# A cross-attention and mixture-of-experts kernel: GpSimd's descriptor memory set to 2048 bytes per partition

## The reference: what is computed

```python
x = x + xattn(layernorm(x), ctx, ctx)        # per position: 16x16 scores of heads, softmax, times v
xf = layernorm(x).reshape(-1, 256)           # 4096 rows
top1 = argmax(xf @ gate_w.T + gate_b)        # one of 8 experts
for e in range(8):
    y = relu(xf @ w1[e].T + b1[e]) @ w2[e].T + b2[e]      # 256 -> 1024 -> 256
    out = out + where(top1 == e, y, 0)
return x + out
```

## Time and profile before

| | us |
|---|---|
| median of 3 runs | 479.29 |
| lowest and highest run | 477.44, 480.28 |
| profiled execution, time | 473.75 |
| profiled execution, span | 471.9 |
| GpSimd busy in it | 214.6 |

### The profile page before, as it was taken

How to read it: one execution, slowest core, us unless ns; L and a number is a source line. 1 busy time by engine, 2 the same in 40 slices (tenths; PEclk the granted TensorE clock), 3 DMA queues, 4 the chain that set the end, 5 groups by cost and what they waited for, 6 DMA issues and landing times.

```text
span 471.9 us, 16303 instructions
## 1 busy us (share of the span) xinstructions
PE 387.6 (82%) x5889; PEld 328.7 (70%) x5889; DVE 338.2 (72%) x777; ACT 179.3 (38%) x317; POOL 214.6 (45%) x213
## 2 busy tenths in 40 slices
PE   0127877997798779884899999888999999999992
PEld 0026767986698779874887777666777877787771
DVE  8789798789882974379539787576576776677671
ACT  2334445444443522245424342333333334333320
POOL 8535453634773558523342545553333523333422
PEclk9999999955557555565589999999999999999997
DMA  7999989989778767657734434666343345644310
GB/s 274 404 244 243 243 218 246 261 204 242 175 180 211 163 137 173 140 134 214 180 86 62 101 92 112 170 193 117 92 102 86 91 99 94 103 86 93 85 51 0
DMA packets 125802, 73.17 MB, mean 155 GB/s; under 512 B 99229, under 2 KB 110238, under 8 KB 125216
## 3 DMA queue, kind: packets, MB, share of 16 engines
q1 hardware_dynamic: 96336, 60.46, 50.4%
q0 software_dynamic: 3408, 8.46, 5.8%
q10 hardware_dynamic: 25984, 3.21, 4.7%
HBM read 48.28 MB, written 11.24 MB: 126 GB/s over the span
## 4 chain that ended last, share of the span: by engine, by line
PE 50%; DVE 11%; DMA 10%; issue 9%; SPq 8%; POOL 7%; ACT 2%; another core or an unknown queue 1%; POOLq 0%; DVEq 0%; ACTq 0%
PE s_ps L1506 15%; PE s_ps L1403 5%; PE at_ps L1522 5%; PE pv_ps L1433 5%; PE lg_ps L1459 5%; PE pv_ps L1522 5%; DMA arena<-qv_hl 4%; DMA arena<-sorted_rows 3%; SPq L601 3%; PE at_ps L1523 3%; PE pv_ps L1523 2%; PE tr_ps L1445 2%; POOL sorted_rows L1340 2%; PE at_ps L1420 2%; DVE arena L1186 2%
## 5 line engine op out<-in xcount | busy, mean ns | idle before, releaser
L1506 PEld LDWEIGHTS s_ps<-arena 128*128 x1872 | 131.9, 99 | 49.4 <-issue 13.4
L1506 PE MATMUL s_ps<-arena 128*128 128x128 f16 x1872 | 157.8, 221 | 6.5 <-issue 3.7
L1366 POOL DMA_INDIRECT result<-arena x39 | 41.2, 1057 | 109.4 <-DVE arena L1228 102.9
L1203 DVE SCALAR_TENSOR_TENSOR arena<-arena,s_ps 128x512 f32<-128x512 f32 x78 | 53.2, 682 | 28.7 <-PE s_ps L1506 10.9
L1433 PE MATMUL pv_ps<-a_hl,arena 128*128 128x16 f16 x1536 | 54.6, 181 | 19.5 <-DMA arena<-qv_hl 14.6
L1433 PEld LDWEIGHTS pv_ps<-a_hl,arena 128*128 128x128 f16 x1536 | 53.4, 118 | 23.0 <-DMA arena<-qv_hl 19.0
L1403 PEld LDWEIGHTS s_ps<-k_hl,arena 128*128 128x128 f16 x1536 | 54.4, 118 | 14.7 <-DMA arena<-qv_hl 10.2
L1522 PE MATMUL at_ps<-arena,k_in 128*128 x160 | 60.6, 383 | 2.5 <-DVE k_hl L1214 2.5
L1403 PE MATMUL s_ps<-k_hl,arena 128*128 128x16 f16 x1536 | 54.1, 181 | 9.3 <-DMA arena<-qv_hl 9.3
L1522 PE MATMUL pv_ps<-arena,x_in 128*128 x152 | 57.3, 379 | 2.5 <-DVE x_in L1214 2.5
L1186 DVE SCALAR_TENSOR_TENSOR arena<-arena 128x512 f16<-128x512 f32 x56 | 47.7, 872 | 0.9 <-ACT arena L863 0.9
(11 more groups left out here) (141 smaller groups left out, 593.5 us busy)
## 6 DMA issues: line engine op xcount, KB each, us to landing
arena<-w SPq DMA_DIRECT2D x28, 512.0 KB, 5.6
arena<-sorted_rows SPq DMA_DIRECT2D x39, 130.0 KB
arena<-b SPq DMA_DIRECT2D x39, 128.0 KB
arena<-qv_hl SPq DMA_DIRECT2D x70, 64.0 KB
k_in<-k_t SPq DMA_DIRECT2D x16, 256.0 KB
arena<-x SPq DMA_DIRECT2D x4, 1024.0 KB, 10.5
x_in<-x_t SPq DMA_DIRECT2D x16, 256.0 KB, 4.7
v_in<-v_t SPq DMA_DIRECT2D x16, 256.0 KB
```

Of the source, the lines that this page charges most:

```text
L1203: eng.scalar_tensor_tensor(out=h_in[:, c].rearrange("p (k t) -> p k t", t=P), in0=bias, scalar=W_SCALE, in1=h_ps[c][:].rearrange("p (k t) ...
L1366: eng.indirect_dma_start(out=out, out_offset=bass.IndirectOffsetOnAxis(ap=rows[:, r, :].bitcast(I32)[:, D + 2:D + 3], axis=0), in_=rows[:, ...
L1506: k = eng.matmul(o, weights_of(j, w + k_ * H + n * P, P), xt[:, j % XB, a + k_], start=(k_, w, a) == (0, HI_1, 0), stop=k_ == KD - 1 and w ...
```

## The change

One argument is added where the program object is made. It sets the descriptor memory to 2048 bytes per partition in place of the default. No instruction is added, removed or moved on any engine (3584 rows of TensorE's queue, 667 of VectorE's, 330 of ScalarE's, 177 of GpSimd's and 544 of SyncE's are the same before and after). What the freed part of SBUF held isn't used for anything else; the tiles behind it get lower addresses.

```diff
@@ -1552,7 +1552,7 @@
         "b2": lay(L0_ffn_b2),
     }
-    nc = bacc.Bacc("TRN2", target_bir_lowering=False, num_devices=1)
+    nc = bacc.Bacc("TRN2", target_bir_lowering=False, num_devices=1, dynamic_dma_scratch_size=2048)
```

## The result

The changed kernel is 1.1% faster: ratio 0.9887 to the kernel before, 95% interval 0.9858 to 0.9917. Its median is 472.22 us (15 runs, 468.13 to 475.56), against 476.62 us (15 runs, 474.28 to 480.28) for the kernel before. The three runs of before that stood ahead of the prediction were thus on the high side.

The account below looks back on a forecast made before the run. TensorE was taken as the main bound (busy 82%, half of the chain), GpSimd only in short places. Instructions, waits for room, bookkeeping and addresses at 0 us each left the median of 479.3 us, range 475.0 to 483.0.

Parts of the forecast that it names:

- the account of the path behind the last store: End of the kernel: the last store at 464.81 us is followed by nothing but its landing; no other cost counted.
- The sum: Whole kernel: 473.75 us profiled plus four terms of 0 us; the change of 0 put on the median, 479.3 us.
- Nothing grows with use: GpSimd's transfers: durations stay level (third 0.97 us, 23rd 0.98, last 0.97), which speaks against a saving; 0 taken.
- The third rival: GpSimd's transfers on the path: large memory costs something now; 0.30 us saved on each of 13, 475.4 us; chance 0.07.
- The first rival: GpSimd's transfers: giving memory back piece by piece costs 1.5 to 4.9 us, plus up to 2.4; 482.8 us; chance 0.16.
- the cover that the prediction had named: Ahead of GpSimd's 39 stores: idle time waiting for VectorE, 102.9 us in sum, hides bookkeeping there.
- Waits for room: GpSimd's scatters: 0 us forecast; as second rival, room for one transfer costs 26.8 us, giving 506.1 us; chance 0.04.
- the estimate of 14: Descriptor memory: 2048 bytes hold 128 descriptors of 16 B, 14 transfers at 9 per engine and side; no wait, 0 us.
- The limit: Scatters in a row: room for four transfers makes none wait, three cost 0.4 us at worst, only two or one bite.
- Addresses: All tiles start lower in SBUF: 0 us taken, bounds -0.30 and +0.30 us a transfer; unforeseen effects 0.01 either side.
- The fourth rival: Whole kernel: the change does nothing, the memory not being as said or read; 479.3 us; chance 0.71 together with the forecast.
- The range: Whole kernel's time: 475.0 to 483.0 us, low end from the saving and the profiled 473.75, high end from bookkeeping's middle.

Follow-up runs that it names:

- e3_small_padded: Kernel before with descriptor memory of 2048 bytes and an unused tile of 14336 bytes per partition, so all tiles keep their addresses; ratio 0.9896 to before.

## Why the prediction was wrong, point by point

**The step that failed** is the account of the path behind the last store: "the last store at 464.81, which nothing follows but its landing". The same rows held the contradiction. A landing takes 2.1 to 4.5 us, so the store would have landed by 469.3 us at the latest (it did by 466.9), and the span ended at 471.9. At least 2.6 us at the end of the program had no owner in the prediction, and I didn't ask whose they were. The trace of before had the owner: GpSimd's drain, 7068 ns from 464.6 us (L383). The sum thus put at nothing what a smaller list saves there. The runs showed 0.08 us for each of the 71 transfers that the large memory had never given back, and a tail 4.3 us shorter at 2048 bytes.

**"Nothing grows with use"**, the argument against a saving, was read from the transfers' durations, and they don't grow: 0.97 us first and last. What grows is the list, and in the kernel before it is paid for once, at the end. The step looked for the price at each transfer, where it would be shown, and not at the place where the list is closed.

**The third rival** (faster, the large memory costs something now) had the sign and by accident nearly the size, 3.9 us against a tail 4.3 us shorter. Its mechanism, a pause of 0.30 us saved on each of 13 transfers, didn't occur: the pauses between scatters stayed at 0.30 us. That the sum came near is luck. Its chance of 0.07 was too low, since the profile had an unexplained stretch that it could have been tied to.

**The first rival** (giving back costs GpSimd time) named a step that exists, but at 2048 bytes it costs nothing that can be told from the run-to-run scatter. It shows as waits that nothing explains ahead of the 27th and the 58th transfer, 0.5 us longer together than before. In the seven kernels whose memory never runs out no transfer has such a wait of over 0.7 us, so they come from the small memory. They lie ahead of stores, where GpSimd waited for VectorE anyway, which is the cover that the prediction had named. With 10176 bytes 1.0 us of it did stand on the path, ahead of the last store. The kernel as a whole lost nothing by it that shows: it gained 3.3 to 7.0 us, and the tail 4.3.

**Waits for room** at 2048 bytes: as good as none, as forecast (0.8 us ahead of one scatter in one of four profiles), and the size of a transfer behind the estimate of 14 holds. The limit was wrong. By the distances I had three transfers of room cost 0.4 us at worst; 512 bytes cost some 10 us, since a transfer without room waits for more than the oldest one. At one transfer I had 26.8 us and 506.1 us; it was 516.06.

**Addresses**: 0 as far as can be told, as forecast. **The fourth rival** (the argument does nothing) is refuted: e3_small_padded changes nothing else but an unused tile.

**The range** began at 475.0 us. 2.7 us of the miss come from the median that I started from, 479.29 us of three runs, where 15 runs have 476.62; even from 479.29 the measured ratio gives 473.9, so the range was too narrow on that side for a gain of 4.3 us at the end.

## What to carry to other kernels

Account for the end of a program: take the last store's start, add its landing, and ask who owns what is left of the span; the drains behind the last line are in the trace. If GpSimd issues many transfers (here 71 indirect ones), the drain at the end goes over each that its descriptor memory still holds, some 0.08 us apiece, and a memory sized for about 14 of them, or one drain in a place where GpSimd idles anyway, moves that cost to where it is hidden. Don't size it for only a few: at three transfers' room this kernel lost 2%, at one 8.5%.

## What the runs showed of the hardware that I had not expected

- A drain on GpSimd takes 0.08 us for each of its transfers still held, from 32 to 71 of them, in the middle of the program (51) as at its end, although all but the last few had landed long before; the floor is 2.6 us from the last store's start.
- When room runs out, giving back is cheaper than by a drain: 1.0 us for a lump of some 37 transfers (their number is read from the tail), 0.03 us apiece, against 0.08 us.
- With 8192 to 10176 bytes room comes back in lumps, and at 512 bytes a transfer that finds none waits past the oldest one's landing: 5.09 us with room for three.
- Whole runs of one program scatter over 468.1 to 475.6 us, but the tail repeats within 0.1 us (7.1, 7.1, 7.1, 7.0 with room for all; 2.8, 2.8, 2.8 with 2048 bytes), so one profile is enough for it where the total needs a dozen runs.
